# Cross-attention scores: two fp32r parts of q and k in two 64-row tiles in place of six bf16 products

## The chip, the cores and the metric

The kernel is one launch on one core of a Trainium2 chip. The metric is the device time of that launch in microseconds (us). Engines: TensorE (PE; its weight loads are shown apart as PEld), VectorE (DVE), ScalarE (ACT), GpSimd (POOL), and SyncE (SP), which here issues every DMA. TensorE writes PSUM, which has eight banks of 512 fp32 values in each of 128 partitions.

## The reference

A decoder layer in fp32 on x of 8 x 512 x 256 (batch, tokens, channels) with a context of 8 x 1601 x 256: a retention block, a cross attention, and a gated feed-forward block with experts, each behind a layer norm and added to x. The change touches the cross attention alone:

```
q = ln(x) @ Wq.T + bq;  k = ctx @ Wk.T + bk;  v = ctx @ Wv.T + bv     # 16 heads of 16
scores = q k^T / sqrt(16)                                              # 512 x 1601 per head and batch
out = softmax(scores) v;  x = x + out @ Wo.T + bo
```

## The kernel before

Three stages run one after the other: retention (to about 346 us), cross attention (to about 2040 us), feed-forward. In the cross attention the work goes batch by batch (8), in each batch group by group (G = 4 groups of GH = 4 heads), in each group chunk by chunk (SC = 13 chunks of up to 128 context rows). Batch 0 ("first") and batch 7 ("last") are written out, batches 1 to 6 ("mid") are one hardware loop.

**Scores.** q and k are split into three bf16 parts each. A head's stationary and moving operands stack six products of parts (KPARTS, QPARTS; 6 x 16 = 96 partitions), so one matmul gives a score to nearly fp32. Three more partitions (MR) hold ones for k and the parts of minus the row maximum for q, so that the score matmul of 99 rows also subtracts the maximum before the exponential. The tiles are kst (per group) and qst.

**In a chunk** TensorE computes, for each pair of heads, two score matmuls (L891) into two PSUM banks; ScalarE makes the exponentials of both in one instruction (L925); TensorE multiplies those of the chunk before by v (values, L864: four heads side by side in column tiles 32 wide, two passes each). The rest of TensorE's work is a list of items, which `fill` places between: two after the first pair, one after the second, the rest after the values.

**Items.** Each item writes one of three work banks (W_BANKS) in turn and waits until the bank's former item is drained by VectorE (`drained`). Most items are maxima of the next group: a matmul of 96 rows and 512 context columns (L811) whose row maximum VectorE takes (L1049), 48 in a group, and four `tails` for the last 65 columns (L816, L1052). Chunks 0 to 7 hold five of them, 8 to 10 four; chunk 11 holds `shift`. Others, placed by `work_of`: `k` (projection of 512 columns; in groups 1 and 2 at chunks 1, 3, 6, 8), `v`, `q`, `xnT`, `norm`, `oT`, `wo`.

```
                            if c != SC - 2:
                                fill(g, plan[g][c][0:2] if pair == 0 else plan[g][c][2:3])
                        if c:
                            values(g, c - 1)
                        fill(g, plan[g][c] if c == SC - 2 else plan[g][c][3:])
```

**Shift.** When all maxima of a group are in, VectorE takes minus their maximum (L1011) and splits it in three bf16 parts (L1013 to L1016), TensorE transposes the parts (L820), VectorE copies them out as rows (mrows, L1057), and SP copies the rows into the q operand, one DMA of three rows per head (`load_shift`, L734). The group's first score matmul waits for them (m_loaded).

**Splitting and spilling.** VectorE adds the bias to a finished q or k item twice: once as bf16 part 0 (L1003) and once whole in fp32 (L1006, tile rest, two buffers). POOL makes the other two parts (`split`, L687, L688, L690); in the prologue VectorE does this itself. kp and qp hold the parts of one batch; SP writes them to DRAM (`spill_q`, `spill_k` per half f of the channels) and reads them back into qst and kst (`load_group`, 12 DMAs for a group, each into 16 partitions), all on the one SP queue. The prologue computes batch 0's q, k, v and the maxima of its first group before any score.

Of the kernel before, what the change touches and what calls it, by code (L numbers as in the profile page):

```python
# [16 lines left out]
F32 = mybir.dt.float32  # L17
BF16 = mybir.dt.bfloat16
F32R = mybir.dt.float32r
ALU = mybir.AluOpType  # L20
# [591 lines left out]
X_LINKS = 22  # L612
# [3 lines left out]
def cross_attention(nc, x_all, ln2, io):  # L616

    assert N_MID % W_BANKS == 0
    with ExitStack() as ctx:
# [9 lines left out]
        identb = sb("x_identb", [P, P], BF16)  # L629
# [3 lines left out]
        kst = [sb(f"x_kst{g}", [XR + MR, GH, S], BF16) for g in range(G)]  # L633
        qst = [sb(f"x_qst{g}", [XR + MR, GH, T], BF16) for g in range(G)]
# [3 lines left out]
        kp = sb("x_kp", [P, KT, 3, S], BF16)  # L638
        qp = sb("x_qp", [P, KT, 3, T], BF16)
        rest = sb("x_rest", [P, 2, 512])  # L640
        left = sb("x_left", [P, 512])
# [7 lines left out]
        negm = sb("x_negm", [P, GH, TT])  # L649
        mres = sb("x_mres", [P, GH, TT])  # L650
        mparts = sb("x_mparts", [P, TT, GH, MR], BF16)
        mrows = sb("x_mrows", [GH * MR, T], BF16)
        rden = sb("x_rden", [P, TT, GH])
        k_dram = nc.dram_tensor("k_parts", [B, KT, 3, P, S], BF16, kind="Internal").ap()
        q_dram = nc.dram_tensor("q_parts", [B, KT, 3, P, T], BF16, kind="Internal").ap()

        consts, ctx_loaded, ones_set = sem("x_consts"), sem("ctx_loaded"), sem("ones_set")
        ones_loaded = sem("ones_loaded")
# [3 lines left out]
        xn_ready, mparts_ready, m_loaded = sem("x_xn_ready"), sem("mparts_ready"), sem("m_loaded")  # L662
# [6 lines left out]
        KQ = 16 * 2 * NB  # L669
# [12 lines left out]

        def split(engine, ops, dst, b1, n, count, w):
# [12 lines left out]
        def _(sp):  # L696
# [8 lines left out]
            def spill_q(b):  # L705
                sp.wait_ge(split_done, b * SPLITS + KT)
                sp.dma_start(q_dram[b].rearrange("k j p t -> p (k j) t"),
                             qp[:].rearrange("p k j t -> p (k j) t")).then_inc(q_spilled, 16)

            def spill_k(b, f):  # L710
                sp.wait_ge(split_done, b * SPLITS + KT + (f + 1) * len(COLS))
                sp.dma_start(k_dram[b, f].rearrange("j p t -> p j t"), kp[:, f]).then_inc(k_spilled[f], 16)
# [962 lines left out]
```

## Time and profile before

| | us |
|---|---|
| runs: median (lowest to highest of 3) | 2491.51 (2489.76 to 2494.42) |
| profiled execution: span, first to last instruction | 2495.0 |
| busy in the span: PE / DVE / ACT / POOL | 2250.3 / 1717.6 / 1033.0 / 452.9 |
| cross attention: prologue, to the first scores | 345.9 to 447.5 |
| one batch inside the loop (scores at 1057.5 to 1263.8) | 206.3 |

The profiled execution has no time of its own beside its span. PE durations are modelled and overlap: what a matmul costs is read from the distance of starts. "Idle <-releaser" names what ended an engine's wait. PEclk is the granted clock of TensorE, 1.00 for 2.4 GHz and 0.50 for 1.2 GHz.

### The profile page before, as it was taken

What the parts mean: (1) busy time and instruction counts of PE and PEld (TensorE: products, weight loads), DVE (VectorE), ACT (ScalarE), POOL (GpSimd) and SP (SyncE); (2) the same over time, 40 slices, a digit from 0 to 9 for tenths busy, and PEclk for the clock granted to TensorE, in tenths of its full rate; (3) what the DMA queues carried; (4) which work ended last, traced back from release to release, by engine and by line L of the source; (5) the groups of instructions that cost most, each with busy time, mean ns of one, the idle gap of its engine ahead of it and who ended that gap; (6) DMA issues with size and microseconds to landing.
All of it is one profiled execution on the core that took longest, in us unless ns stands there. A gap on an engine that the chain in (4) does not pass through costs nothing. (4 is left out here: it accounts for less than half of the span.)

```text
span 2495.0 us, 39210 instructions
## 1 busy us (share of the span) xinstructions
PE 2250.3 (90%) x12690; PEld 1091.7 (44%) x12690; DVE 1717.6 (69%) x3336; ACT 1033.0 (41%) x1177; POOL 452.9 (18%) x419
## 2 busy tenths in 40 slices
PE   6889858889999998998998999999899978899999
PEld 4665633233333333333333333333333227777777
DVE  6888859778877787787876778778787837612121
ACT  2222300445544544554554555454455653222222
POOL 1110101121121121112012112112101005232222
PEclk9999977899999999999999999999999988899999
DMA  3000027242223204224223320431421001000000
GB/s 105 1 0 0 0 51 139 52 79 47 54 60 67 61 14 85 63 39 73 47 55 71 62 54 18 89 70 25 73 47 28 1 12 55 0 9 11 14 17 17
DMA packets 61919, 110.06 MB, mean 44 GB/s; under 512 B 9236, under 2 KB 40340, under 8 KB 61596
## 3 DMA queue, kind: packets, MB, share of 16 engines
q1 hardware_dynamic: 61736, 107.80, 20.6%
q8 instruction: 93, 1.52, 0.3%
q14 instruction: 90, 0.74, 0.1%
HBM read 77.21 MB, written 30.16 MB: 43 GB/s over the span
## 5 line engine op out<-in xcount | busy, mean ns | idle before, releaser
L925 ACT ACTIVATE x_probs<-x_ps 128x1024 f32<-128x1024 f32 (+1 forms) x832 | 831.0, 1022 | 859.3 <-PE x_ps L891 853.7
L1049 DVE TENSOR_REDUCE x_mx<-x_ps 128x1 f32<-128x512 f32 x1536 | 958.0, 682 | 131.0 <-PE x_ps L811 125.5
L811 PE MATMUL x_ps<-x_kst,x_qst 96*128 96x512 bf16 x1536 | 555.1, 401 | 43.2 <-DVE x_mx L1049 39.7
L891 PE MATMUL x_ps<-x_qst,x_kst 99*128 99x512 bf16 (+1 forms) x1664 | 506.5, 391 | 68.0 <-DMA x_qst<-x_mrows 51.2
L864 PE MATMUL x_ps<-x_probs,x_vst 128*17 128x512 f32 (+1 forms) x3328 | 437.9, 598 | 9.7 <-ACT x_probs L925 7.1
L811 PEld LDWEIGHTS x_ps<-x_kst,x_qst 96*128 96x128 bf16 x1536 | 140.5, 99 | 513.1 <-DVE x_mx L1049 376.6
L891 PEld LDWEIGHTS x_ps<-x_qst,x_kst 99*128 99x128 bf16 (+1 forms) x1664 | 161.2, 101 | 241.8 <-issue 101.6
L1480 DVE TENSOR_TENSOR f_hid_whole<-f_ps,f_act_g 128x512 f32<-128x512 f32 x80 | 55.3, 691 | 258.2 <-PE f_ps L1237 250.1
L1352 ACT ACTIVATE f_act_g<-f_ps 128x512 f32<-128x512 f32 x80 | 47.8, 598 | 263.5 <-PE f_ps L1268 251.6
L1418 POOL TENSOR_TENSOR f_hid_rest<-f_hid_whole,f_hid_rounded 128x512 fp32r<-128x512 f32 x80 | 103.4, 1293 | 250.0 <-ACT f_hid_rounded L1358 250.0
L951 POOL TENSOR_TENSOR x_vst<-x_v_all,x_bv 128x768 f32<-128x768 f32 x64 | 65.8, 1063 | 449.3 <-DVE x_v_all L1045 392.8
L687 POOL TENSOR_TENSOR x_kp<-x_rest,x_kp 128x512 bf16<-128x512 f32 (+1 forms) x56 | 53.1, 949 | 455.6 <-DVE x_rest L1006 455.6
L864 PEld LDWEIGHTS x_ps<-x_probs,x_vst 128*17 128x17 f32 (+1 forms) x3328 | 55.1, 95 | 173.7 <-issue 104.1
L212 PE MATMUL r_ps<-r_qwide,r_kT 128*128 128x512 f32 x256 | 116.2, 602 | 10.0 <-DVE r_vz L438 10.0
L283 ACT ACTIVATE r_qwide<-r_qT,r_headmask 128x512 f32<-128x512 f32 x128 | 80.0, 709 | 105.0 <-DVE r_qT L432 105.0
L800 PE MATMUL x_ps<-x_ctxT,x_wk 128*128 128x512 f32 (+1 forms) x256 | 105.2, 536 | 4.0 <-DVE x_rest L1006 3.7
L807 PE MATMUL x_ps<-x_wv,x_ctxT 128*128 128x256 f32 (+1 forms) x416 | 104.2, 392 | 2.8 <-DVE x_rest L1006 2.8
L447 DVE TENSOR_TENSOR r_probs<-r_ps,r_decay 128x512 f32<-128x512 f32 x128 | 84.5, 687 | 22.2 <-PE r_ps L212 21.4
L1282 PE MATMUL f_ps<-f_wd_rounded,f_hid_rest 128*128 128x256 f32 x320 | 91.2, 285 | 7.7 <-POOL f_hid_rest L1418 4.2
L1282 PE MATMUL f_ps<-f_wd_rounded,f_hid_rounded 128*128 128x256 f32 x320 | 91.2, 285 | 0.0
L1282 PE MATMUL f_ps<-f_wd_rest,f_hid_rounded 128*128 128x256 f32 x320 | 91.1, 285 | 0.0
L1089 DVE COPY x_ou<-x_ps 128x512 f32<-128x512 f32 x32 | 22.1, 692 | 93.0 <-PE x_ps L864 93.0
(196 smaller groups left out, 2561.6 us busy)
## 6 DMA issues: line engine op xcount, KB each, us to landing
x_kst<-k_parts SPq DMA_DIRECT2D x192, 200.1 KB, 8.2
k_parts<-x_kp SPq DMA_DIRECT2D x16, 1200.8 KB, 4.6
x_ctxT<-in_ctxT SPq DMA_DIRECT2D x8, 1601.0 KB, 7.7
x_qst<-q_parts SPq DMA_DIRECT2D x192, 64.0 KB, 2.4
q_parts<-x_qp SPq DMA_DIRECT2D x8, 768.0 KB, 3.6
x_all<-in_x SPq DMA_DIRECT2D x8, 512.0 KB, 3.9
out<-x_all SPq DMA_DIRECT2D x8, 512.0 KB, 2.9
x_qst<-x_mrows SPq DMA_DIRECT2D x128, 3.0 KB
```

Of the source, the lines that this page charges most:

```text
L212: pe.matmul(ps[:, o, :], kT[:, f, c * P:(c + 1) * P], qwide[:, f, 4 * half:4 * half + 4, c * P:(c + 1) * P], start=True, stop=True).then_i ...
L283: ins = nc.scalar.activation(qwide[:, f, h, :], qT[:, f, :], ACT.Copy, scale=headmask[:, h:h + 1])
L447: nc.vector.tensor_tensor(probs[:, c % 2, h:h + 4, :], ps[:, item(), :].rearrange("p (h t) -> p h t", h=4), decay[:, h:h + 4, :], ALU.mult ...
L800: m = pe.matmul(o[:, 0:w], wk[:, kk, item[1] * P:(item[1] + 1) * P], ctxT[:, kk, c:c + w], start=kk == 0, stop=kk == KT - 1)
L807: m = pe.matmul(o[0:w, (c - c0) * D:(c - c0 + 1) * D], ctxT[:, kk, c * P:c * P + w], wv[:, kk, :], start=kk == 0, stop=kk == KT - 1)
L811: m = pe.matmul(o, qst[g][0:XR, j, t * P:(t + 1) * P], kst[g][0:XR, j, i * 512:(i + 1) * 512], start=True, stop=True)
L864: m = pe.matmul(ps[32 * j:32 * j + HD + 1, PV, :], vst[g][0:w, q, j, :], probs[0:w, slot, j % 2, :], start=q == 0, stop=q == SC - 1)
L891: m = pe.matmul(ps[0:w, 2 * (n % 2) + h, :], kst[g][:, 2 * pair + h, c * P:c * P + w], qst[g][:, 2 * pair + h, :], start=True, stop=True)
L925: nc.scalar.activation(probs[0:w, n % 4, :, :], ps[0:w, 2 * (n % 2):2 * (n % 2) + 2, :], ACT.Exp, scale=HD ** -0.5).then_inc(exp_done, 1)
L1049: ins = nc.vector.tensor_reduce(out=mx[:, j, t, i:i + 1], in_=o, axis=AX.X, op=ALU.max)
L1282: m = pe.matmul(ps[:, DOWN + t // 2, (t % 2) * D:(t % 2 + 1) * D], hid[l][:, buf, t * P:(t + 1) * P], wd[r][:, j, :], start=start and n == ...
L1418: nc.gpsimd.tensor_tensor(hid[1][:, buf, :], hid_whole[:, buf, :], hid[0][:, buf, :], ALU.subtract).then_inc(hid_split, 1)
```

## The change

- q and k are split into two parts of type fp32r (the rounded value and the rest). An operand stacks three products (48 partitions) and two rows for the maximum (MR = 2): 50 rows, in a tile of 64. Two heads of a pair lie at partitions 0 and 64 (`half`) of the same tile, and their score matmuls follow one another. The maxima alternate between the halves. The tail is 66 columns wide (one column is computed twice), so its width is even.
- VectorE adds the bias once (`keep_whole`); POOL (VectorE in the prologue) makes part 0 by adding zero, then the rest. kp holds one half f of the channels, so the split of the second half waits until the first is spilled, and the other way round.
- The shift: minus the maximum is transposed in fp32, VectorE makes both parts from PSUM, and SP copies each row of each head alone: 8 DMAs per group for 4.
- The rows of ones are preset by POOL over all of kst (no DMA); every engine waits for the presets.
- `load_group` still has 12 DMAs; each takes two heads of fp32 where it took four of bf16. A spill of k is two parts of fp32 for three of bf16.

```
-KPARTS = [0, 1, 0, 2, 0, 1]
-QPARTS = [0, 0, 1, 0, 2, 1]
+KPARTS = [1, 0, 0]
+QPARTS = [0, 1, 0]
-MR = 3
+MR = 2
+ROWS = 64
+PAIRS = GH // 2
-TAIL = S - FULL * 512
+TAIL_AT = FULL * 512 - 1
+TAIL = S - TAIL_AT
...
-    for j in range(GH):
-        out += [("max", g, j, t, i) for t in range(TT) for i in range(FULL)] + [("tails", g, j)]
+    for pair in range(PAIRS):
+        out += [("max", g, pair, half, t, i) for t in range(TT) for i in range(FULL) for half in range(2)]
+        out += [("tails", g, pair, half) for half in range(2)]
...
-        kst = [sb(f"x_kst{g}", [XR + MR, GH, S], BF16) for g in range(G)]
-        qst = [sb(f"x_qst{g}", [XR + MR, GH, T], BF16) for g in range(G)]
+        kst = [sb(f"x_kst{g}", [P, PAIRS, S], F32R) for g in range(G)]
+        qst = [sb(f"x_qst{g}", [P, PAIRS, T], F32R) for g in range(G)]
-        kp = sb("x_kp", [P, KT, 3, S], BF16)
+        kp = sb("x_kp", [P, 2, S], F32R)
...
+        def split_k(engine, ops, b1, f, i, count):
+            c, w = COLS[i]
+            if f:
+                engine.wait_ge(k_spilled[0], b1 * 16 + 16)
+            elif not (isinstance(b1, int) and b1 == 0):
+                engine.wait_ge(k_spilled[1], b1 * 16)
+            split(engine, ops, lambda j: kp[:, j, c:c + w], b1, KT + f * len(COLS) + i, count, w)
...
-            ops.tensor_tensor(dst(1), whole, dst(0), ALU.subtract)
-            ops.tensor_tensor(left[:, 0:w], whole, dst(0), ALU.subtract).then_inc(split_step, 1)
+            ops.tensor_tensor(dst(0), whole, zero[:].broadcast_to([P, w]), ALU.add).then_inc(split_step, 1)
             engine.wait_ge(split_step, b1 * SPLITS + (n + 1))
-            ops.tensor_tensor(dst(2), left[:, 0:w], dst(1), ALU.subtract).then_inc(split_done, 1)
+            ops.tensor_tensor(dst(1), whole, dst(0), ALU.subtract).then_inc(split_done, 1)
...
+                    for half in range(2):
+                        for n, part in enumerate(parts):
+                            at = half * ROWS + n * HD
+                            rows = src[b, f, part, lo:lo + GH * HD, :].rearrange("(j h d) c -> h d j c", h=2, d=HD)
+                            sp.dma_start(dst[at:at + HD, :, :].bitcast(F32), rows[half]).then_inc(kq_loaded[g], 16)
...
                 for j in range(GH):
-                    sp.dma_start(qst[g][XR:XR + MR, j, :], mrows[j * MR:(j + 1) * MR, :]).then_inc(m_loaded, 16)
+                    for part in range(MR):
+                        at = (j % 2) * ROWS + XR + part
+                        sp.dma_start(qst[g][at:at + 1, j // 2, :].bitcast(F32),
+                                     mrows[part][j:j + 1, :].bitcast(F32)).then_inc(m_loaded, 16)
...
+                    rows = slice(half * ROWS, half * ROWS + XR)
+                    m = pe.matmul(o, qst[g][rows, pair, t * P:(t + 1) * P], kst[g][rows, pair, i * 512:(i + 1) * 512],
                                   start=True, stop=True)
...
-                        m = pe.matmul(o[0:GH * MR, t * P:(t + 1) * P], mparts[:, t, :, :], identb[:],
-                                      start=True, stop=True)
+                        m = pe.matmul(o[0:GH, t * P:(t + 1) * P], negm[:, t, :], ident[:], start=True, stop=True)
...
                             for h in range(2):
-                                m = pe.matmul(ps[0:w, 2 * (n % 2) + h, :], kst[g][:, 2 * pair + h, c * P:c * P + w],
-                                              qst[g][:, 2 * pair + h, :], start=True, stop=True)
+                                rows = slice(h * ROWS, h * ROWS + XR + MR)
+                                m = pe.matmul(ps[0:w, 2 * (n % 2) + h, :], kst[g][rows, pair, c * P:c * P + w],
+                                              qst[g][rows, pair, :], start=True, stop=True)
...
+            nc.gpsimd.memset(zero[:], 0.0).then_inc(ones_set, 1)
+            for g in range(G):
+                nc.gpsimd.memset(kst[g][:].bitcast(F32), 1.0).then_inc(ones_set, 1)
...
-                    ins = nc.vector.tensor_copy(mrows[:], o[0:GH * MR, :])
+                        dve.wait_ge(m_loaded, shifts * MLOADS)
+                    link(nc.vector.tensor_copy(mrows[0][:], o[0:GH, :]))
+                    ins = nc.vector.tensor_tensor(mrows[1][:], o[0:GH, :], mrows[0][:], ALU.subtract)
```

## Rows read from the trace of the kernel before

**Rows 1.** The page: busy time, share of the span and instructions of each engine.
```profile
PE 2250.3 (90%) x12690; PEld 1091.7 (44%) x12690; DVE 1717.6 (69%) x3336; ACT 1033.0 (41%) x1177; POOL 452.9 (18%) x419
```

**Rows 2.** Order of time, one chunk: start us, duration us, engine, line, [idle <-releaser].
```profile
1022.24 0.68 DVE L1049 TENSOR_REDUCE x_mx<-x_ps 128x1 f32<-128x512 f32 x1
...
1022.97 0.10 PEld L811 LDWEIGHTS x_ps<-x_kst,x_qst 96*128 96x128 bf16 x1 [0.27 <-DVE x_mx L1049]
1023.04 0.38 PE L811 MATMUL x_ps<-x_kst,x_qst 96*128 96x512 bf16 x1
1023.35 1.05 PE L864 MATMUL x_ps<-x_probs,x_vst 128*17 128x512 f32 x8
...
1024.33 0.11 PEld L811 LDWEIGHTS x_ps<-x_kst,x_qst 96*128 96x128 bf16 x2 [0.85 <-DVE x_mx L1049]
1024.76 1.29 DVE L1049 TENSOR_REDUCE x_mx<-x_ps 128x1 f32<-128x512 f32 x2
```

**Rows 3.** Order of time and engines by stretch (busy, clock, DMA), in the prologue's maxima.
```profile
414.27 7.25 DVE L1049 TENSOR_REDUCE x_mx<-x_ps 128x1 f32<-128x512 f32 x12
...
411.50:436.00 24.50, 23.54 (x54) 4.92 (x54) 24.50 (x44) 0.00 (x0) 3.69 (x4) 0.50 0.89 157
```

**Rows 4.** Order of time: first scores of a four-max chunk and of the next.
```profile
1955.11 0.60 PE L891 MATMUL x_ps<-x_qst,x_kst 99*128 99x512 bf16 x2
...
1957.94 0.60 PE L891 MATMUL x_ps<-x_qst,x_kst 99*128 99x512 bf16 x2
```

**Rows 5.** Order of time: a group boundary of the last batch.
```profile
1962.93 0.68 DVE L1057 CAST x_mrows<-x_ps 12x512 bf16<-12x512 f32 x1 [0.49 <-PE x_ps L820]
...
1963.63 3.08 SPq L734 DMA_DIRECT2D x_qst<-x_mrows  x4
...
1967.85 0.98 PE L891 MATMUL x_ps<-x_qst,x_kst 99*128 99x512 bf16 x2 [1.26 <-DMA x_qst<-x_mrows]
```

**Rows 6.** Order of time, and two lines' weights (ns min/median/max): fp32r against bf16.
```profile
2300.57 0.63 PE L1237 MATMUL f_ps<-f_xnT_rounded,f_wg_rest 128*128 x2
...
L1237 PEld LDWEIGHTS f_ps<-f_xnT_rounded,f_wg_rest x160: 186/192/338, 2068.6 to 2482.1; 128*128 128x128 f32 x160
...
L811 PEld LDWEIGHTS x_ps<-x_kst,x_qst x1536: 95/96/153, 406.3 to 2000.7; 96*128 96x128 bf16 x192
```

**Rows 7.** Order of time on VectorE: a k item and the maxima behind it.
```profile
1124.11 0.75 DVE L1003 TENSOR_SCALAR x_kp<-x_ps,x_bk 128x512 bf16<-128x512 f32 x1 [1.08 <-PE x_ps L800]
...
1125.44 1.88 DVE L1049 TENSOR_REDUCE x_mx<-x_ps 128x1 f32<-128x512 f32 x3
```

**Rows 8.** Two lines of SyncE: issue time, ns min/median/max.
```profile
L734 SPq DMA_DIRECT2D x_qst<-x_mrows x128: 639/641/809, 439.5 to 2007.4; - x128
...
L737 SPq DMA_DIRECT2D x_kst<-in_ones_rows x4: 251/272/392, 350.2 to 351.2; - x4
```

**Rows 9.** Order of time at a boundary of groups 1 to 2; the stretch behind it.
```profile
1144.77 0.41 SPq L712 DMA_DIRECT2D k_parts<-x_kp  x1
...
1165.19 1.03 PE L891 MATMUL x_ps<-x_qst,x_kst 99*128 99x512 bf16 x2 [5.35 <-DMA x_qst<-x_mrows]
...
1165.20:1172.00 6.80, 6.80 (x21) 2.97 (x22) 3.70 (x6) 3.07 (x3) 0.00 (x0) 0.70 1.07 140
```

**Rows 10.** Order of time in the prologue: POOL's presets; a k item, first and last operation.
```profile
345.90 3.16 POOL L935 MEMSET x_vst<- 128x884 f32 x4 [5.75 <-POOLq L53]
...
375.34 0.75 DVE L1003 TENSOR_SCALAR x_kp<-x_ps,x_bk 128x512 bf16<-128x512 f32 x1
...
378.12 0.69 DVE L690 TENSOR_TENSOR x_kp<-x_left,x_kp 128x512 bf16<-128x512 f32 x1
```

**Rows 11.** Order of time: first spill of k and first scores.
```profile
387.01 0.38 SPq L712 DMA_DIRECT2D k_parts<-x_kp  x1
...
447.48 1.04 PE L891 MATMUL x_ps<-x_qst,x_kst 99*128 99x512 bf16 x2 [8.73 <-DMA x_qst<-x_mrows]
```

**Rows 12.** Engines by stretch: PE, PEld, DVE, ACT, POOL busy, clock, DMA; last group.
```profile
2009.00:2034.50 25.50, 23.61 (x140) 4.88 (x140) 0.72 (x3) 22.45 (x24) 0.00 (x0) 1.00 0.00 1
```

More of the change, by code:

```diff
@@ L611 @@
 PREV = N_MID - N_FIRST
-X_LINKS = 22
+X_LINKS = 10
 S_ITEMS = 2 * SC * G
@@ L681, in position, with split_q @@
             return order(plans[kind]).index(item)
+        def split_q(engine, ops, b1, f, count):
+            if not (isinstance(b1, int) and b1 == 0):
+                engine.wait_ge(q_spilled, b1 * 16)
+            split(engine, ops, lambda j: qp[:, f, j, :], b1, f, count, T)
+        def split_k(engine, ops, b1, f, i, count):
[5 more added lines that the diff above has]
+            split(engine, ops, lambda j: kp[:, j, c:c + w], b1, KT + f * len(COLS) + i, count, w)
         def split(engine, ops, dst, b1, n, count, w):
@@ L809, in work @@
                 elif kind == "max":
-                    _, g, j, t, i = item
-                    m = pe.matmul(o, qst[g][0:XR, j, t * P:(t + 1) * P], kst[g][0:XR, j, i * 512:(i + 1) * 512],
+                    _, g, pair, half, t, i = item
+                    rows = slice(half * ROWS, half * ROWS + XR)
+                    m = pe.matmul(o, qst[g][rows, pair, t * P:(t + 1) * P], kst[g][rows, pair, i * 512:(i + 1) * 512],
                                   start=True, stop=True)
                 elif kind == "tails":
-                    _, g, j = item
+                    _, g, pair, half = item
+                    rows = slice(half * ROWS, half * ROWS + XR)
                     for t in range(TT):
-                        m = pe.matmul(o[:, t * TAIL:(t + 1) * TAIL], qst[g][0:XR, j, t * P:(t + 1) * P],
-                                      kst[g][0:XR, j, FULL * 512:S], start=True, stop=True)
+                        m = pe.matmul(o[:, t * TAIL:(t + 1) * TAIL], qst[g][rows, pair, t * P:(t + 1) * P],
+                                      kst[g][rows, pair, TAIL_AT:S], start=True, stop=True)
                 elif kind == "shift":
                     for t in range(TT):
-                        m = pe.matmul(o[0:GH * MR, t * P:(t + 1) * P], mparts[:, t, :, :], identb[:],
-                                      start=True, stop=True)
+                        m = pe.matmul(o[0:GH, t * P:(t + 1) * P], negm[:, t, :], ident[:], start=True, stop=True)
                 elif kind == "norm":
@@ L1029, in work @@
                     f = item[1]
-                    if f == 0 and not (isinstance(b1, int) and b1 == 0):
-                        dve.wait_ge(q_spilled, b1 * 16)
-                    ins = first_part(o, qp[:, f, 0, :], bq[:, f:f + 1], f, b1, T)
+                    ins = keep_whole(o, bq[:, f:f + 1], f, b1, T)
                 elif kind == "k":
@@ L1035, in work @@
                     c, w = COLS[i]
-                    if f == 0 and i == 0 and not (isinstance(b1, int) and b1 == 0):
-                        for part in k_spilled:
-                            dve.wait_ge(part, b1 * 16)
-                    ins = first_part(o, kp[:, f, 0, c:c + w], bk[:, f:f + 1], KT + f * len(COLS) + i, b1, w)
+                    ins = keep_whole(o, bk[:, f:f + 1], KT + f * len(COLS) + i, b1, w)
                 elif kind == "v":
@@ L1047, in work @@
                 elif kind == "max":
-                    _, g, j, t, i = item
+                    _, g, pair, half, t, i = item
+                    j = 2 * pair + half
                     ins = nc.vector.tensor_reduce(out=mx[:, j, t, i:i + 1], in_=o, axis=AX.X, op=ALU.max)
                 elif kind == "tails":
-                    _, g, j = item
+                    _, g, pair, half = item
+                    j = 2 * pair + half
                     ins = nc.vector.tensor_reduce(out=mx[:, j, :, FULL], in_=o[:, 0:TT * TAIL].rearrange("p (t c) -> p t c", t=TT),
@@ L1663 @@
     })
-    arrays["ones_rows"] = np.ones((MR, GH, S), ml_dtypes.bfloat16)
     nc = bacc.Bacc("TRN2", target_bir_lowering=False, num_devices=1)
```

79 lines of the change are left out of this document (31 added, 48 removed).

## Prediction

> **What bounds the kernel now.** I read the page's head, then the order of time inside one chunk of the cross attention, then the boundaries between groups of heads. The page [rows 1] shows TensorE busy 90%, which would promise much for a change that shortens its scores; but matmul durations overlap. In the order of time, two bf16 matmuls that take 0.38 us each end 0.60 us after the first began, so their starts lie 0.22 apart [rows 2, 4]. A chunk with five maxima and nothing else (c = 1 to 7) asks TensorE for 9 x 0.218 + 0.985 (the values) + 0.09 = 3.04 us. It takes 3.13: row maxima on VectorE take 0.598 each when they follow one another (12 in 7.25 us) [rows 3], 2.99 for five.
>
> What really sets the 3.13 is a loop over the three work banks [rows 2]. A maximum starts at 1022.24 and takes 0.68; 0.05 later the weights of matmul M3, which needs its bank, begin (1022.97); the matmul follows at 1023.04, held 0.07 by the scores ahead of it; the values start 0.31 later; M4 0.985 after that; its maximum 0.43 after M4's start; one more maximum (0.598) closes the round. Sum 0.68 + 0.05 + 0.07 + 0.31 + 0.985 + 0.43 + 0.598 = 3.12 us. In chunks with four maxima (c = 8 to 10) the loop lacks that last maximum, 2.53, and TensorE is the bound: scores at 1955.11, the next chunk's at 1957.94, 2.83 us [rows 4]. At a group's end the next scores need the shift rows from the SP queue [rows 5]. So a faster score matmul shortens one term of 0.07 in most chunks, and the rest of the loop is latency.
>
> **The change part by part.** All sums are against the profiled execution: span 2495.0 us. The page gives no time beyond it; the median of the runs is 2491.5, 3.5 less, and I put my difference on the median.
>
> (a) Score and max matmuls, 117 five-max chunks without other work (217 chunks c1 to c7 in the 31 groups that compute maxima, less 42 with a full k item and 58 with another item). In the loop the 0.07 goes. Two fp32r matmuls of 512 columns end 0.63 after the first began, against 0.60 [rows 6, 4]: +0.015 for one. Its weights take 192 ns against 96 in bf16 [rows 6], and M3 and M4 load theirs after the wait they stand behind, in the open: +0.096 twice. Net +0.14 per chunk, +16.3 us. Bounds: weights wholly hidden, -0.05; two row tiles that don't run side by side, +0.17 (third rival). I take the open weights, because M4's weights start at 1024.33 with M4 itself, although bank and data were there since 1023.6 [rows 2].
>
> (b) 93 four-max chunks: TensorE no longer binds, since two scores in different halves of the rows should overlap as the value matmuls do (8 records in 1.05 us [rows 2]). The loop remains, 2.53 + 0.14 = 2.67 against 2.83: -0.16 each, -14.9 us. Bounds -0.36 and +0.19 (rivals).
>
> (c) Chunks with a projection or transpose. These matmuls use all 128 rows, so they now stand between 64-row ones. The trace has no such switch; the nearest is into and out of the 32-column values, 0.09 (0.31 less 0.22) and 0.10. Bounds 0 and 0.1 for each; I take 0.1. The Trainium skill (TensorEngine Tiling (Array Packing), Key Properties) says that a change of tiling mode drains the engine; by that rule each such switch costs the upper bound. Each k item loses one of two VectorE operations (0.67 of 1.33 us [rows 7]), but the maximum of M3 then waits for TensorE: it started at 1126.63; after, from k's end at 1123.9 two openings 0.2, three matmul slots 0.7, 0.09, 0.985 and 0.53 give about 1126.4. -0.2 in 42 chunks, -0.1 in 14 k tails, -10 together. In the other 58 the same sum gives +0.12, +7. Net -3. Bounds +0.35 in each (serial tiles) and -0.4 (nothing open).
>
> (d) Group boundaries. VectorE drops four small operations (0.88 us) and adds a second full-width one with its wait (0.75); the shift matmul becomes fp32, +0.2. About even: 2.5 us from the first operation to the last row, 2.27 to 2.44 now. Then SP issues eight copies of one row, not four of three rows, and TensorE waits for them with ScalarE and VectorE behind it. Four take 2.8 us, 641 ns each [rows 8]; of the one other copy with three rows an issue took 272. Bounds for eight: 2.4 and 5.6 us; I take 5.5, since the 641 has the same source and target. From the end of the shift rows to the next scores it is 3.9 to 4.2 us when nothing else holds (1963.61 to 1967.85 [rows 5]) and becomes about 6.6. In the last batch all three boundaries pay it, 6.2 to 9.1 with the 2.5: +8.7. Into and out of the loop over batches, +2.8 each, +5.6. Groups 0 to 1 and 2 to 3 have projections there, 8.2 us now: +0.9 in 14, +12.6. Groups 3 to 0 inside the loop already take 9.2, through the loop's branch: 0. Groups 1 to 2 wait for the queue: spill at 1144.77, the reload and the shift rows behind it, scores at 1165.19 [rows 9]. The spill is 1600 KB for 1201 in packets twice as long, +0.5 us with the eight rows, in 7 batches +3.5. The reload has as many copies and bytes, each to 16 partitions as now. Sum +30.4; with cheap issues +3.5.
>
> (e) Prologue. Each full q or k item has five VectorE operations, 3.5 us from one item to the next, then three, 2.2: eight items, -10, two tails -1 [rows 10]. Against it kp holds one half only: the first item of the second half waits some 5.5 us for the spill behind the last split. Then the queue decides, as now (first spill 387.01, first scores 447.48 [rows 11]): it starts 7 us earlier and carries 2 more, -4.5 with rounding. POOL presets kst: 884 elements took 0.79 us (3.16 for four [rows 10]), 3202 thus 2.8, 11.3 before the same 3.2; all wait until 360.3, and TensorE started at 361.8 anyway: 0.
>
> (f) The last group has no maxima; TensorE is busy 23.6 and ScalarE 22.5 of 25.5 us [rows 12]: -2.5, down to ScalarE. After each long boundary wait the granted clock falls to its 1.2 GHz level for about 7 us and VectorE starves: clock 0.70, VectorE 3.7 of 6.8 us over such a stretch [rows 9]. With scores side by side that costs 0.5 less in 12, -6, and new such stretches in the last batch take back 3. -5.5 in all.
>
> Sum 16.3 - 14.9 - 3 + 30.4 - 4.5 - 5.5 = +18.8. Forecast 2491.5 + 18.8 = 2510.
>
> **Rivals.** First, the other side: the weights are hidden, M3's and M4's entering one half of the array while the other streams. The loops shorten: -0.05 x 117 = -6, -0.36 x 93 = -33, -23 in (c), +30 and -10 from the rest: -42, 2450. The Trainium skill (TensorE: Matmul & The Clock Gate, Part 3, The mechanism) says that weights are pulled ahead under a running matmul when its row group differs. Against it: M3 and M4 wait before their weights, and nothing runs at 1024.33 that could hide them. It decides from 0.07 us per chunk (18.8 over 268 chunks).
> Second, an issue of one row costs as the 272 ns ones. Without the 27 us the sum is -8, 2483. For it: two kinds of three-row copy differ by more than twice. Against: source and target on the chip are as now.
> Third, the change doesn't do what it says: the halves run one after the other. No 64-row tile is in the trace. TensorE then needs 9 x 0.235 + 1.08 + 0.1 = 3.3 in a five-max chunk (+20), 3.02 for 2.83 in 93 (+18), +35 in (c), +30 - 4.5: +100, 2590.
> Fourth, TensorE streams less and its clock falls. It fell at 411.5 us, where a 512-column matmul came every 0.6 us, and stayed low [rows 3]; in the later chunks it would have 0.47 of scores, 1.18 of maxima and 0.86 of values in 3.26 us. Loops at 1.2 GHz would add nearly 1 us each, 2750. Little speaks for it.
>
> **How the numbers follow.** Forecast 0.42, hidden weights 0.20, cheap issues 0.13, serial halves 0.15, clock 0.03, mixtures 0.07. A difference under 0.2% (5 us) can't be told from none. Slower: forecast, serial, clock and a part of the rest, 0.60. Faster: hidden weights and most of cheap issues, 0.29. Same 0.11. The forecast's own range is 2495 to 2530; the 8 in 10 range is 2447 to 2588, from the first rival's price to the third's.
>
> **What would show it.** Scores of a pair starting within 0.02 us (right) or 0.23 apart (third rival). Five-max chunks at 3.26 (right), 3.07 or less (first). M4's weights starting with M4. Eight SP issues of 0.64 us before each group, and TensorE waiting for them over 3 us in the last batch (right), or 0.3 us each (second). The clock full outside the boundaries. The first spill some 7 us earlier. Any of these at the rival's value makes the forecast wrong by its price.

## The result and the profile after

The changed kernel takes 2676.4 us (median of 4 runs, 2674.5 to 2696.0) against 2491.6 for the kernel before on the same chip: 1.076 times, 95% interval 1.073 to 1.080. The forecast was 2510. Slower was right, the size was not: +185 us in place of +19, outside the range. Times are medians of the executions within 1.5% of the fastest of the same kernel; only the run with 51 rows below had others, two of its four.

The page of the changed kernel, to be read against [rows 1]:

```profile
PE 2367.6 (89%) x12818; PEld 1243.2 (47%) x12818; DVE 1675.0 (63%) x3150; ACT 1038.1 (39%) x1177; POOL 398.1 (15%) x353
...
PEclk9999976898877888888988889898899987989999
```

TensorE has 117 us more busy time, VectorE 43 less and POOL 55 less. The last row is the granted clock in 40 slices: eights where the attention runs. Engines by stretch, attention alone (first to last exponential; the columns are those of [rows 3]), first the kernel before, then the changed one:

```profile
449.00:2038.00 1589.00, 1479.02 (x8086) 530.13 (x8087) 1216.00 (x2171) 830.55 (x832) 260.83 (x266) 0.97 0.25 51
```

```profile
444.00:2217.00 1773.00, 1599.78 (x8206) 673.45 (x8202) 1182.72 (x2008) 835.89 (x832) 195.62 (x196) 0.87 0.24 50
1028.90:1042.60 13.70, 12.89 (x69) 4.47 (x68) 11.74 (x21) 6.89 (x7) 4.63 (x4) 1.00 0.01 2
1042.60:1049.40 6.80, 6.80 (x36) 2.87 (x28) 3.91 (x8) 2.32 (x3) 0.00 (x0) 0.50 0.00 0
1063.10:1090.40 27.30, 24.72 (x149) 12.03 (x145) 17.80 (x31) 13.71 (x14) 0.00 (x0) 1.00 0.47 99
```

The mean granted clock went from 0.97 to 0.87. It has two levels only, so a mean of 0.87 over 1773 us is about 450 us at 1.2 GHz (summed from the record of the clock: 448.5 us, in 50 falls; before 99.5 us, in 13). The last three rows are stretches of one batch. At 1.00 VectorE is busy 11.7 of 13.7 us and 17.8 of 27.3. In the 6.8 us at 0.50 TensorE is busy all the time and VectorE 3.9: it waits for matmuls. This fall does not stand behind a long wait: TensorE was busy 12.89 of the 13.70 us ahead of it. Of the 13 falls before, 12 begin between 4 us ahead and 7 us behind a group's first scores; of the 50 now, 25 do. Score and maximum matmuls are as many as before, but 48 or 50 rows high instead of 96 or 99, and of fp32r instead of bf16.

Order of time in one five-maximum chunk at full clock (start, duration, what ended the idle time):

```profile
1031.80 0.50 PE L830 MATMUL x_ps<-x_kst,x_qst 48*128 48x512 f32 x1 [0.56 <-DVE x_mx L1059]
1031.88 0.64 PE L911 MATMUL x_ps<-x_qst,x_kst 50*128 50x512 f32 x2
...
1034.02 1.05 PE L883 MATMUL x_ps<-x_probs,x_vst 128*17 128x512 f32 x8
```

The first score matmul starts 0.085 us behind a maximum of the other half: that overlap exists. The second starts at 1032.138 (the two together last 0.64), 0.25 behind the first, which is the third rival's sign (0.23) and not the forecast's (0.02). Over the trace both occur: of 554 pairs in chunks at full clock 151 start within 0.02 us of each other and 380 stand 0.20 to 0.36 apart; in the kernel before all stand over 0.20 apart.

Order of time at a boundary of the last batch, against [rows 5]:

```profile
2086.03 0.68 DVE L1069 TENSOR_TENSOR x_mrows<-x_ps,x_mrows 4x512 fp32r<-4x512 f32 x1
2086.74 4.93 SPq L753 DMA_DIRECT2D x_qst<-x_mrows  x8
...
2092.85 0.79 PE L911 MATMUL x_ps<-x_qst,x_kst 50*128 50x512 f32 x2 [4.04 <-DMA x_qst<-x_mrows]
```

Eight issues take 4.93 us, 0.62 each (the median of all 256 is 0.59; the 128 of three rows before had 0.64), and TensorE waits 4.04 us where it waited 1.26.

Chunk 11 of a group, whose item is the shift; before, then after:

```profile
1001.14 0.30 PE L816 MATMUL x_ps<-x_kst,x_qst 96*128 96x65 bf16 x4
1001.27 1.03 PE L891 MATMUL x_ps<-x_qst,x_kst 99*128 99x512 bf16 x4
...
1003.17 0.38 PE L820 MATMUL x_ps<-x_identb,x_mparts 128*12 128x128 bf16 x4
...
1005.31 0.60 PE L891 MATMUL x_ps<-x_qst,x_kst 99*65 99x512 bf16 x2
```

```profile
1068.89 0.50 PE L911 MATMUL x_ps<-x_qst,x_kst 50*128 50x512 f32 x1
...
1069.34 0.70 PE L911 MATMUL x_ps<-x_qst,x_kst 50*128 50x512 f32 x2
1069.97 1.05 PE L883 MATMUL x_ps<-x_probs,x_vst 128*17 128x512 f32 x8
...
1070.84 1.04 PE L840 MATMUL x_ps<-x_ident,x_negm 128*4 128x128 f32 x8
1071.81 1.99 PE L825 MATMUL x_ps<-x_wv,x_ctxT 128*128 128x256 f32 x8
...
1073.73 0.44 PE L911 MATMUL x_ps<-x_qst,x_kst 50*65 50x512 f32 x2
```

From the chunk's first scores (1001.27 and 1068.89) to the next chunk's: 4.04 us, now 4.84. The shift item was four bf16 matmuls in 0.38 us. It is now four fp32 ones, which the trace shows as eight records (called passes here) in 1.04 us, in TensorE's order, with everything behind them.

**Where the 184.4 us of the attention went.** From first scores to the last group's last chunk the trace has 1587.4 and 1771.8 us. For each kind of chunk I took its time at full clock (median of those with no half clock, with the runs below that have the same instructions where the changed kernel has none) and split:

| part | before | after | difference |
|---|---|---|---|
| chunks 0 to 10 at full clock | 1246.6 | 1245.2 | -1.4 |
| chunk 11 at full clock | 113.6 | 140.2 | +26.6 |
| chunks 0 to 11, above full clock | 29.9 | 149.2 | +119.3 |
| chunk 12 with the group boundary | 197.3 | 237.2 | +39.9 |

The first three rows rest on medians per kind of chunk and are good to a few us. The prologue gives back 4.5 (first scores 447.5, now 443.0), what follows the attention 2. That makes 178, the difference of the two spans (2495.0 and 2672.7); the medians differ by 185, because the execution profiled before is slower than the median of its kernel and the one profiled after is faster.

### The profile page after: what moved, and what is told of

Same layout as the page of the kernel before. It is cut to its first block and busy times, and to the rows that moved or that the text cites. A ratio compares the mean times of both kernels' runs of the same rounds, so it can differ in the third digit from the quotient of the medians.

```text
span 2672.7 us, 39381 instructions
## 1 busy us (share of the span) xinstructions
PE 2367.6 (89%) x12818; PEld 1243.2 (47%) x12818; DVE 1675.0 (63%) x3150; ACT 1038.1 (39%) x1177; POOL 398.1 (15%) x353
## 5 line engine op out<-in xcount | busy, mean ns | idle before, releaser
L830 PE MATMUL x_ps<-x_kst,x_qst 48*128 48x512 f32 x1536 | 630.3, 524 | 58.8 <-DVE x_mx L1059 45.0
L911 PE MATMUL x_ps<-x_qst,x_kst 50*128 50x512 f32 (+1 forms) x1664 | 532.1, 482 | 109.9 <-DMA x_qst<-x_mrows 107.6
L830 PEld LDWEIGHTS x_ps<-x_kst,x_qst 48*128 48x128 f32 x1536 | 261.9, 206 | 575.5 <-DVE x_mx L1059 522.0
L883 PE MATMUL x_ps<-x_probs,x_vst 128*17 128x512 f32 (+1 forms) x3328 | 482.9, 655 | 12.2 <-ACT x_probs L945 9.4
L911 PEld LDWEIGHTS x_ps<-x_qst,x_kst 50*128 50x128 f32 (+1 forms) x1664 | 225.1, 205 | 186.6 <-issue 122.1
L704 POOL TENSOR_TENSOR x_kp<-x_rest,x_zero 128x512 fp32r<-128x512 f32 (+1 forms) x56 | 47.7, 852 | 585.2 <-DVE x_rest L1025 585.2
L818 PE MATMUL x_ps<-x_ctxT,x_wk 128*128 128x512 f32 (+1 forms) x256 | 132.6, 655 | 0.6 <-DVE x_rest L1025 0.6
L825 PE MATMUL x_ps<-x_wv,x_ctxT 128*128 128x256 f32 (+1 forms) x416 | 115.9, 424 | 5.8 <-DVE x_rest L1025 5.8
L825 PEld LDWEIGHTS x_ps<-x_wv,x_ctxT 128*128 128x128 f32 (+1 forms) x416 | 79.9, 203 | 34.4 <-issue 10.0
L836 PEld LDWEIGHTS x_ps<-x_kst,x_qst 48*128 48x128 f32 x512 | 73.2, 210 | 48.9 <-DVE x_mx L1063 25.5
```

What stands on the lines that cost most here:

```text
L818: m = pe.matmul(o[:, 0:w], wk[:, kk, item[1] * P:(item[1] + 1) * P], ctxT[:, kk, c:c + w], start=kk == 0, stop=kk == KT - 1)
L825: m = pe.matmul(o[0:w, (c - c0) * D:(c - c0 + 1) * D], ctxT[:, kk, c * P:c * P + w], wv[:, kk, :], start=kk == 0, stop=kk == KT - 1)
L830: m = pe.matmul(o, qst[g][rows, pair, t * P:(t + 1) * P], kst[g][rows, pair, i * 512:(i + 1) * 512], start=True, stop=True)
L883: m = pe.matmul(ps[32 * j:32 * j + HD + 1, PV, :], vst[g][0:w, q, j, :], probs[0:w, slot, j % 2, :], start=q == 0, stop=q == SC - 1)
L911: m = pe.matmul(ps[0:w, 2 * (n % 2) + h, :], kst[g][rows, pair, c * P:c * P + w], qst[g][rows, pair, :], start=True, stop=True)
```

## The experiments

Half clock below is the time at 1.2 GHz within the attention, summed from each trace. It is that of the one profiled execution. For the others it can be estimated from their mean clock and span, with the half clock outside the attention taken from the trace: 431 to 505 us in the changed kernel (449 in its trace), 54 to 90 in the kernel before, whose trace, with 99, lies above them all. So differences of some 50 us (20 where there is little of it) can't be told in one trace. Waits are TensorE's ahead of each group's first scores (66 us before, 108 in the changed kernel). Ratios are to the kernel before in the same session, with 95% intervals.

**Full rows, no tiles.** fp32r stays; one matmul covers both heads' rows (it computes the sum of two heads' scores, not each).
```
-rows = slice(half * ROWS, half * ROWS + XR)
+rows = slice(0, ALL)                       # 112
```


> Every score and max matmul takes 114 or 112 rows of the same fp32r operands (both heads at once), so there is no 64-row tile; the result is that of the sum of two heads' scores, all the rest is the changed kernel. Theory A (matmuls in half of the rows are what lets the clock fall, 449 us of the attention at half clock): the time at half clock falls below 150 us, five-max chunks stay near 3.3 us and four-max ones rise to 3.0; about 2590 us. Rival B (fp32r operands let it fall, or the boundary waits do): half clock stays at 400 us or more and the time rises to 2690 or more through serial matmuls.

Measured: 2663.7 us, ratio 1.068 [1.066, 1.071]. Half clock 127 us, waits 111, but plain five-maximum chunks at full clock take 3.61 us on average (116 of them) against 3.41 in the tiles (79). With 112 rows at work the half clock falls from 449 to 127 us with the same number of matmuls, as theory A had it. The time does not follow, as rival B had it: the chunks are longer at full clock. That is what the tiles give, and the full rows give back the clock; here the two come out nearly even (2663.7 against 2676.4). Whether the longer chunks are serial streaming or weights in the open was not told apart.

**bf16 in the tiles.** The same structure, parts and shift rows in bf16.
```
-kst = [sb(f"x_kst{g}", [P, PAIRS, S], F32R) for g in range(G)]
+kst = [sb(f"x_kst{g}", [P, PAIRS, S], BF16) for g in range(G)]
```


> The changed kernel with both parts, the shift rows and their copies in bf16 (less precise scores, half the bytes): 64-row tiles stay, fp32r goes. Theory A: the clock stays low (350 us or more at half clock), but weights load fast, so five-max chunks at full clock take 3.1 and the tails cost 0.5 less: about 2600 us. Rival B: half clock below 150 us and about 2500 us.

Measured: 2483.9 us, ratio 0.998 [0.996, 1.000]. Half clock 229 us, waits 79. Plain five-maximum chunks 3.16 us on average, chunk 11 4.40, and the groups 1 to 2 boundary chunk inside the loop, which waits for the reload of half the bytes, 6.4 us against 9.9. The weights take 94 ns, not 186. Neither expectation had the clock: at the same rows, tiles and order the bf16 operands take away half of the half clock (449 to 229 us), so rows alone do not set it. The edit also halves the bytes and shortens waits (108 to 79); which of these lifts the clock this run alone does not tell.

**One shift row.** The changed kernel with one fp32r row per head: four copies, one VectorE operation less.
```
-MR = 2
+MR = 1
```


> The changed kernel with one shift row for two (the row maximum rounded to fp32r once, the same in numerator and denominator), so four copies per group for eight and one VectorE operation less in the shift. Theory C (the eight issues cost what they show, 0.62 us each, in every boundary): the wait before a group falls by 2.5 to 3.3 us in the last batch and at groups 3 to 0, by 1 us at groups 0 to 1 and 2 to 3; about -45 us in all, 2632. Rival: the boundary is held by the tails and the shift matmul, -10 us, 2666.

Measured: 2617.0 us, ratio 1.049 [1.045, 1.054]. All chunks 12 together fall from 237.2 to 192.6 us, back to the 197.3 of before; waits from 108 to 65 us. Half clock is 466 us in the trace, but that is of the slowest execution (2645.6 us); the other three (2607 to 2624) come to an estimated 347, 374 and 419. So the waits are not the main cause of the 449 us; a share of some 50 can't be excluded.

**All 64 rows in use.** The changed kernel with the maximum over 62 rows and the scores over 64 of each tile; the added rows of q are zero.
```
+XT = 62
-rows = slice(half * ROWS, half * ROWS + XR)
+rows = slice(half * ROWS, half * ROWS + XT)
```


> The changed kernel with 62 rows (maxima) and 64 rows (scores) in each 64-row tile, the rows added being zero in q, for 48 and 50. No instruction more. If the count of rows in use lets the clock fall, half clock falls from 449 to under 350 us and the time to about 2630; if it is the halves themselves or anything else, 2676 within 5 us.

Measured: 2624.9 us, ratio 1.053 [1.050, 1.057]. Half clock 273 us, with waits at 120. (Four presets of q on POOL put the first scores 5 us later, at 448.1.) Engines by stretch, the attention with one shift row, then with 64 rows:

```profile
446.00:2188.00 1742.00, 1613.44 (x8212) 677.21 (x8212) 1159.46 (x1977) 836.64 (x832) 196.02 (x196) 0.87 0.24 51
```

```profile
449.00:2163.00 1714.00, 1524.76 (x8206) 647.69 (x8204) 1179.11 (x2008) 835.84 (x832) 195.63 (x196) 0.92 0.25 52
```

The one shift row leaves the clock at 0.87 in its (slowest) execution; more rows, on the same matmuls and with no shorter waits, lift it to 0.92. The added rows hold zeros in q and ones in k.

**Both of these at once.**
```
+XT = 63
-MR = 2
+MR = 1
```


> The changed kernel with both earlier edits at once: every score and maximum matmul over all 64 rows of its tile (added rows of q are zero), and one row for the shift, so four one-row copies instead of eight. Theory 'clock and boundaries are separate terms': the two gains add up, 59 us for the copies and 52 us for the rows, so 2566 us (2550 to 2585), with 64 us of waits ahead of the groups as with one row, and 250 to 300 us of half clock in the attention. What then is left over the kernel before, some 75 us, is neither clock fall nor copies. Rival 'the clock falls because the boundaries idle the engine': the rows and the shorter boundaries take away the same falls, so the gains overlap, and the time stays near 2600 us (2590 to 2620).

Measured: 2547.8 us, ratio 1.024 [1.021, 1.027]; half clock 204 us, waits 67. The gains add up and a little more (129 us; 59 + 52 = 111); the time lies just below the 2550 to 2585 expected. The rival, overlapping gains, is out. Against the run with two shift rows and 64 rows the waits halve (120 to 67) and half clock goes from 273 to 204: the waits have a share in fp32r too. What fp32r tiles then lose to the kernel before, 56 us, is chunk 11 (27) and the rest of the clock (time above full clock 62.5 us against 29.9).

**The same in bf16** (one shift row, 63 and 64 rows): the bf16 kernel above with
```
+XT = 63
-MR = 2
+MR = 1
```


> The 64-row tiles with two parts in bf16 (2483.9 us in its own run, 229 us of half clock, 79 us of waits ahead of the groups), and with one shift row and all 64 rows of each tile in use. Theory 'rows in use set the clock': the half clock in the attention falls to 110 to 150 us; at 0.29 us won per us of half clock, as the rows gave in fp32r, that is 25 to 35 us, and the boundaries give 25 to 30 us more (waits near 50 us): 2430 us (2415 to 2445). Rival 'in bf16 VectorE sets the chunks and the clock costs nothing': only the boundaries' share, 2455 to 2465 us, whatever the clock does. Second rival, the rows do nothing in bf16: half clock stays at 220 to 240 us, 2455 us.

Measured: 2372.4 us, ratio 0.953 [0.950, 0.955], below all three expectations. Half clock 83 us, waits 24. Against the fp32r kernel of the same form (2547.8) chunks 0 to 11 at full clock take 1297 us instead of 1385, the time above that is 22 instead of 62, and the chunks 12 take 155 instead of 197, all of it in the groups 1 to 2 boundary that waits for bytes. Half clock at the same rows and tiles: 204 in fp32r, 83 in bf16.

**The kernel before with half the rows.** Three products per head: the same instructions over 48 and 51 rows; the smaller products are left out.
```
-KPARTS = [0, 1, 0, 2, 0, 1]
-QPARTS = [0, 0, 1, 0, 2, 1]
+KPARTS = [1, 0, 0]
+QPARTS = [0, 1, 0]
```


> The kernel before, with three bf16 products per head in place of six: a score matmul is 51 rows high instead of 99 and a maximum matmul 48 instead of 96; the instructions, their order and their columns are the same, only the DMAs that fill q and k are six per group instead of twelve. It leaves out the smaller products. Theory 'rows in use set the clock': half clock in the attention rises from 100 us to 230 us or more, and the time by 0.1 to 0.29 us for each us of it, 2505 to 2535 us. Rival 'the clock fell in the changed kernel for the fp32r reads, the tiles or the boundaries': the half clock stays at 80 to 120 us and the time at 2480 to 2492 us.

Measured: 2700 and 2738 us, 208 and 246 us slower than the kernel before (2492.0); with two values there is no interval, but the gap is far beyond the spread. Its attention, in the execution of 2738:

```profile
445.00:2279.00 1834.00, 1774.65 (x8086) 558.51 (x8088) 1231.13 (x2171) 834.35 (x832) 260.56 (x266) 0.82 0.13 32
```

Half clock 646 us, waits down to 21, no fp32r, no tile, no second shift copy. The direction was expected, the size not (2505 to 2535). Take half the rows out of the same matmuls, and the old kernel loses more than the changed one did, although it has half the bytes to reload.

**Maxima half by half**, not in turn.
```
-out += [("max", g, pair, half, t, i) for t in range(TT) for i in range(FULL) for half in range(2)]
-out += [("tails", g, pair, half) for half in range(2)]
+for half in range(2):
+    out += [("max", g, pair, half, t, i) for t in range(TT) for i in range(FULL)] + [("tails", g, pair, half)]
```


> The changed kernel with the next group's maxima in another order: all maxima and the tails of one half of the array, then those of the other, not in turn. Neighbouring maxima then share a tile, and the two tails items are 17 maxima apart. Theory A, as the prediction had it: a score matmul starts 85 ns after a maximum of the other half and 250 ns after one of its own, so on average half the chunks lose 0.165 us twice; five-maximum chunks go from 3.23 to about 3.4 us in part of the groups, +15 to +40 us, 2690 to 2715 us. Theory B: VectorE sets most of these chunks, the order costs nothing there, and chunk 11 gets back the 0.8 us that two adjacent tails items cost it: 31 times 0.4 to 0.8 us, 2650 to 2665 us. The half clock stays at 400 to 480 us in both.

Measured: 2894.6 us, ratio 1.162 [1.157, 1.167]; half clock 959 us. Both theories missed the size. At full clock chunks 0 to 11 of group 2 take 45.9 us against 44.7 (k chunks 5.08 against 4.52, some others less), an estimated 38 us over 31 groups: within theory A's 15 to 40 for the overlap across halves. Chunk 11 stays at 4.84, so adjacent tails are not its loss (theory B is out). The larger part is again the clock.

**The same order with all 64 rows.**
```
+XT = 62
-rows = slice(half * ROWS, half * ROWS + XR)
+rows = slice(half * ROWS, half * ROWS + XT)
```


> The fp32r kernel with the maxima half by half (2894.6 us, 960 us of half clock) with all 64 rows of each tile in use. Theory 'the clock goes by the rows at work, and neighbouring matmuls of one half leave the other idle': more rows help here too, but not to what they give in the alternating order: half clock 450 to 650 us, 2720 to 2800 us. Rival 'the order costs by its serial matmuls, the clock only by the rows': half clock near the 273 us of the alternating order, 2650 to 2690 us. Rival 'the order alone keeps the clock down': half clock over 850 us, 2860 us or more.

Measured: 2668.9 us, ratio 1.072 [1.069, 1.075], half clock 322 us: in the range of the rival that the order costs by its serial matmuls and the clock goes by the rows. Why the order alone doubled the half clock at 48 rows stays open.

**The kernel before with one shift row.**
```
-MR = 3
+MR = 1
```


> The kernel before with one bf16 row for the shift instead of three: a shift item has one VectorE conversion where it had four operations in a row, and each of its four copies moves one row, not three; the six products per head stay. Question: how much of the gain of the 64-row bf16 tiles with one shift row (2372.4 us) has nothing to do with tiles. Theory 'the tiles carry it': the shorter shift item takes at most 0.6 us from each of 31 last chunks and waits ahead of the groups fall from 66 to some 50 us, 2465 to 2485 us. Rival 'the one row carries it': waits fall to 24 us as there, and the time to 2400 to 2440 us.

Measured: 2494.2 us, ratio 1.001 [1.000, 1.003]. Neither theory: chunk 11 goes from 4.03 to 3.97 us, the four issues stay (0.58 us each where three rows took 0.64), and no time is won. So one shift row alone is not the gain of the bf16 kernels. It lies in the tiles and in what came with them (half the bytes in the reload, one VectorE operation less in a k item), which no run takes apart.

**Two copies per shift** in the bf16 kernel, each for both heads of a half.
```
-for j in range(GH):
-    sp.dma_start(qst[g][at:at + 1, j // 2, :], mrows[part][j:j + 1, :]).then_inc(m_loaded, 16)
+for half in range(2):
+    sp.dma_start(qst[g][at:at + 1, :, :], mrows[0][half * PAIRS:(half + 1) * PAIRS, :]).then_inc(m_loaded, 16)
```


> The 64-row bf16 tiles with one shift row and all rows in use (2372.4 us), with two one-row copies per shift, each for both heads of one half, not four: two issues of some 0.6 us less on SyncE between the shift and the next group. Theory 'issues are on the path only where a group waits': of 24 us of waits ahead of the groups 8 to 14 us go, 2358 to 2366 us. Rival 'the landing, not the issue, ends the wait': less than 3 us, 2370 to 2374 us.

Measured: 2379.9 us, ratio 0.955 [0.953, 0.957]: no gain. The last chunks of groups 0 to 2 shorten by 0.9 us in the last batch (4.41 to 3.49) and not at all in the others (4.76); the one through the loop's branch took 9.7 us in this trace and 6.8 in the other, which I can't explain.

**bf16 tiles, one shift row, 48 and 49 rows**: the first bf16 kernel with
```
-MR = 2
+MR = 1
```


> The 64-row bf16 tiles with one shift row, but 48 (maximum) and 49 (score) rows of each tile in use: one edit less than the kernel of 2372.4 us, one more than that of 2483.9 us. Theory 'both edits carry the gain': waits ahead of the groups fall from 79 us to near 30 us and the half clock stays at 170 to 230 us; 2425 to 2440 us, so that the rows in use are worth 50 to 70 us and the shorter boundary about the same. Rival 'the half clock came from the waits': with them gone it falls near 84 us as well, 2375 to 2395 us.

Measured: 2393.3 us, ratio 0.961 [0.959, 0.963]; half clock 121 us, waits 22. Of the 111 us between the two bf16 kernels above the boundary carries 91, the rows 21. Here the shorter waits lowered the half clock (229 to 121) and the time fell into the rival's range: in bf16 a good part of the half clock hung on the waits. With 48 and 49 rows in tiles it is then near that of the kernel before on 96 and 99 (99); without tiles, on 48 and 51 rows, it was 646.

**The kernel before over all 128 rows**, added rows zero.
```
+XT = 125
-m = pe.matmul(o, qst[g][0:XR, j, ...
+m = pe.matmul(o, qst[g][0:XT, j, ...
```


> The kernel before with its score and maximum matmuls over all 128 rows in place of 99 and 96; the added rows of q are zero, nothing else changes. Theory 'rows in use set the clock': of its 100 us of half clock in the attention most goes, and at the 0.28 us lost per us of half clock beyond full-clock times that the kernel before shows (about 30 us of chunk time, and c12 besides) the time is 2462 to 2478 us. Rival 'above some 96 rows the rows no longer matter; what half clock is left comes from the waits ahead of the groups': no change, 2486 to 2495 us, half clock 85 to 105 us.

Measured: 2510.2 us, ratio 1.008 [1.007, 1.010]: slower, as neither theory said. The traces show half clock of 99.5 and 66.5 us and an attention of 1589.0 and 1577.4. But the first is of a slow execution of its kernel and the second of the fastest of its own; over all executions both kernels come to an estimated median of 80 us of half clock. So no effect of the rows is shown above 96. POOL's presets of q and k, with those of v, now hold TensorE at the start. First and last of the twelve presets:

```profile
345.54 0.83 POOL L937 MEMSET x_vst<- 128x884 f32 x1 [5.75 <-POOLq L53]
346.31 5.43 POOL L938 MEMSET x_kst<- 128x6404 bf16 x1
...
375.96 1.80 POOL L939 MEMSET x_qst<- 128x2048 bf16 x1
```

First scores come at 473.3 instead of 447.5, 26 us later, for 19 us in all; so about 7 us are won elsewhere, and the run does not say by what.

**The shift matmul in bf16**, in the fastest kernel.
```
-m = pe.matmul(o[0:GH, t * P:(t + 1) * P], negm[:, t, :], ident[:], start=True, stop=True)
+m = pe.matmul(o[0:GH, t * P:(t + 1) * P], negm[:, t, :], identb[:], start=True, stop=True)
```


> The fastest kernel so far (64-row bf16 tiles, one shift row, all rows in use, 2372.4 us), with its shift matmuls in bf16: four of 128 columns in place of eight passes of fp32, 55 ns apart in place of 109 ns. Theory 'chunk 11 is long by the order on TensorE: whatever the shift item takes there is on the path': chunk 11 falls from 4.40 to 3.7 to 3.8 us in each of 31 groups, 2350 to 2356 us; then 0.65 of the 0.8 us that chunk 11 gained in the changed kernel was the fp32 shift matmul. Rival 'VectorE ends chunk 11': chunk 11 falls by less than 0.2 us, 2366 to 2374 us.

The tile negm is bf16 here as well.

Measured: 2349.0 us, ratio 0.944 [0.942, 0.947]. Chunk 11 falls from 4.40 to 3.75 us, as the first theory had it:

```profile
938.58 0.39 PE L842 MATMUL x_ps<-x_identb,x_negm 128*4 128x128 bf16 x4
```

The shift item takes 0.39 us where it took 1.04. This kernel is 5.6% faster than the kernel before and 12% faster than the changed one, with the less precise bf16 scores.

## Why the forecast was wrong

**The clock is the step that failed.** The forecast gave it a net of -3 us within (f) (-6 for falls that cost less, +3 for new ones in the last batch) and called the rest a rival: "Fourth, TensorE streams less and its clock falls ... Little speaks for it", a chance of 0.03; its sign was "The clock full outside the boundaries". Measured is 449 us at 1.2 GHz for 99, half of the falls away from the boundaries, and +119 of the 178 us between the two traces. It was argued by how long matmuls stream, and by that measure nothing changed: TensorE is busy 90 and 89% in the two pages. What changed is rows and type of the matmuls:

| rows of a maximum / score | type | 64-row tiles | half clock, us | waits, us |
|---|---|---|---|---|
| 96 / 99 (before) | bf16 | no | 99 | 66 |
| 48 / 51 | bf16 | no | 646 | 21 |
| 112 / 114 | fp32r | no | 127 | 111 |
| 48 / 50 (changed) | fp32r | yes | 449 | 108 |
| 62 / 64 | fp32r | yes | 273 | 120 |
| 48 / 50, maxima half by half | fp32r | yes | 959 | 91 |
| 62 / 64, maxima half by half | fp32r | yes | 322 | 120 |
| 48 / 49, one shift row | fp32r | yes | 466 (others 347 to 419) | 65 |
| 63 / 64, one shift row | fp32r | yes | 204 | 67 |
| 48 / 50 | bf16 | yes | 229 | 79 |
| 48 / 49, one shift row | bf16 | yes | 121 | 22 |
| 63 / 64, one shift row | bf16 | yes | 83 | 24 |

Three pairs with the matmuls and their order alike show the rows: 48 to 62 in the tile, 449 to 273 us; the same with the maxima half by half, 959 to 322; 96 to 48 in the kernel before, 99 to 646. The type has an effect as large at the same rows and tiles (449 to 229, 204 to 83). Its runs also move half the bytes and wait less, but waits don't explain it: bf16 with 79 us of them has 229, fp32r with 65 has 347 to 466. In bf16 half height cost 646 us without tiles and 229 or 121 in them. Shorter waits take 108 us off in bf16 on 48 rows, and 69 in fp32r on 64. So the changed kernel lost its clock by half-height matmuls in fp32r together, with a smaller share of the waits; how rows, type, tiles and order combine stays open.

The Trainium skill (TensorE: Matmul & The Clock Gate, What's actually happening) says that the gate goes by how busy the engine has been recently. Read as time spent streaming, this does not agree: the trace shows TensorE busy 12.89 of 13.70 us ahead of a fall and 6.80 of 6.80 us at half clock. Even the rival was too dear at its own terms: it had all chunks near 1 us longer, and what was measured is 119.3 us for 335 us more of half clock in chunks 0 to 11, 0.36 us lost for each.

**(a) Right in the mean.** The 117 plain five-maximum chunks cost about 0.16 us more each at full clock, +18.3 us; forecast 0.14 and +16.3. The mean hides several kinds: chunks 3 and 6 of group 3 went from 3.13 to 3.28 (forecast 3.26), chunk 5 of groups 1 and 2 from 3.13 to 3.02, the first rival's value, and chunk 2 of group 0 in the loop from 3.42 to 3.89. **(b) Wrong by 21 us.** The 93 four-maximum chunks cost +6.5, not -14.9. Chunk 9 of groups 0 and 3 does take 2.68, as forecast (2.67); chunk 8 (up to 3.54) and chunk 10 with its two tails items (2.83 against 2.74) do not. **(c) Wrong by 17 the other way.** 28 k chunks gain 0.74 each, not 0.2; the 14 that share a transpose item gain nothing; -19.6 in all for a forecast of -3. Chunk 0, which had no term, gains 8. (a) to (c) come to +5.2 for a forecast of -1.6, and all chunks 0 to 10 to -1.4: near by cancelling, which is luck.

**(d) The boundaries: right in kind, 10 us short, and one term missing.** 0.62 us per issue (4.93 for eight, forecast 5.5) and +2.8 in the last batch (2.9) are near the forecast; groups 0 to 1 and 2 to 3 pay 1.03 (0.9). What failed here is "Groups 3 to 0 inside the loop already take 9.2, through the loop's branch: 0". The two add up: chunk 12 there goes from 6.76 to 9.48 us in five passes, 14 in all. Groups 1 to 2 paid nothing in the loop (10.4, now 9.9), for a forecast of +3.5. Missing was chunk 11: "the shift matmul becomes fp32, +0.2. About even" was a statement on latency, and the price is on TensorE's own order, +0.86 us in 31 groups, 26.6 us. The last experiment puts 0.65 of it on the fp32 passes; the bf16 tiles put 0.44 on fp32r tails and scores (4.84 to 4.40). That is 0.2 too much; the four dropped VectorE operations may give it back, but no run shows it (three of them dropped in the kernel before gave 0.06). **(e) Right**, -4.5. **(f)** The last group did not shorten (25.7, now 27.3 us).

The first rival (hidden weights) is out as a whole by (a), though chunk 5 behaves as it says. The weights took 186 ns in fp32r and 94 in bf16; the Trainium skill (TensorE: Matmul & The Clock Gate, Weight-path perf modes — Fast Weight Load (FWL) and DoubleRow) says that the fast weight load is off for fp32 inputs, and the trace agrees. The second (cheap issues) is out by the 0.62 us. The third (serial halves) is half right: most pairs of scores start 0.20 to 0.36 us apart, but 151 of 554 start together, and the first of a pair can start 0.085 behind a maximum of the other half. Its price for plain five-maximum chunks (+20) is as near to the measured 18.3 as the forecast's 16.3.

## What to carry to other kernels

Before cutting the contraction of matmuls that are issued without pause, count the rows that stay in use: a kernel at 0.97 of full clock on 96 rows lost 8 to 10% when the same matmuls used 48. The type counts as well: the same tiles had 449 us of half clock in fp32r and 229 in bf16. If rows of a 64-row tile are free, fill them with zeros, and put the preset where nothing waits for it. An item that costs VectorE nothing more can still cost TensorE, which works in order: price each small matmul where it stands there, and use a one-pass type for it where the values allow. Read the clock of every execution, not of the profiled one alone, before a change in it is called an effect.

## What the runs showed of the hardware that was not expected

- Rows whose products are zero count as rows in use: the padding held zeros of q against ones of k, and the half clock fell from 449 to 273 us.
- The edit from fp32r to bf16 operands moves the clock: at the same rows, tiles and order 449 us of half clock in fp32r and 229 in bf16, with longer waits (79 us) than an fp32r run that has 347 to 466 (65).
- With 48-row tiles the order of the halves alone moved the half clock from 449 to 959 us, at 64 rows from 273 to 322. No run says why.
- Four fp32 matmuls with 4 columns of weights over 128 columns of data are eight passes 0.109 us apart (1.04 us in all); in bf16 they are four, 0.055 apart (0.39 us).
- Issuing a copy of one row within the on-chip memory took SyncE 0.58 to 0.59 us (medians), little less than the 0.64 of three rows, and the kernel before did not gain by it (2494.2 us against 2491.1).
